# The prefix of a fused attention and feed-forward kernel: transposes on TensorE, another order of its turns, and background tiles placed otherwise

## The chip, the cores and the metric

The kernel runs on the 8 cores of one Trainium2 chip, as one program with other data on each core and no exchange between them. Time is device time of the slowest core, in microseconds (us). A profile is one profiled execution, and its page and trace show the slowest core of it, here core 6, unless another is named. The engines are TensorE (PE; its weight loads are PEld), VectorE (DVE), ScalarE (ACT), GpSimd (POOL) and the sync engine (SP), which only issues DMAs.

## What is computed

A layer on x of shape 4 x 4096 x 1024: layer norm, then a gated recurrence over time (heads of 256), whose result is normalised and multiplied by Wo, plus a feed-forward block with ternary weights; both are added to x.

```python
xn = _layernorm(x)
q, k, v = silu(xn @ Wq.T), silu(xn @ Wk.T), silu(xn @ Wv.T)
f = log_sigmoid(xn @ Wf.T) / 8;  s = 1 - exp(f)
S1[t] = S1[t-1] * exp(f) + k s^T ;  qv = softmax(q S1)
S2[t] = S2[t-1] * exp(f) + s v^T ;  o  = silu(qv S2)
attn = rms_norm(o) * g_w @ Wo.T
ffn  = bitlinear(silu(bitlinear(xn, w_gate)) * bitlinear(xn, w_up), w_down)
out  = x + attn + ffn        # bitlinear: weights to {-1,0,1} times their mean |w|
```

Time is a recurrence, so a core that has the second half of a sequence needs the states S1 and S2 after the first half. Each core owns 2048 rows (`xr`) and has the 2048 rows before them (`xp`; zeros for the first half), from which it computes the states itself. This is the prefix. All weights come as float32 in HBM.

## The kernel before

Rows are worked in tiles of 128: NP = 16 tiles of the prefix, from the last to the first, then NO = 16 own tiles. The program is written as one list of operations for each engine (a `Lane`), in the order in which the Python code calls them, with semaphore waits where an operation needs another's result; each engine plays its list strictly in order. So the place of a call in the code is its place in each engine's queue. `mm` and `tr` are matmul and transpose on TensorE, `act` ScalarE, `ts`, `stt`, `tt` and `cp(dv, ...)` VectorE, `cp(gp, ...)` GpSimd, `dma` and `dmaT` (transpose) DMAs of the sync queue, except those that name `gp`.

Stage A1 (from line 518; the loop at 561, 17 steps, called turns): `ln_load` loads a tile of xp into one of two buffers `xin`; `ln_stats` and `ln_rstd` give mean and 1/std (VectorE, then two tiny ScalarE steps); `a_apply` (539) calls `ln_apply` (364), which normalises to bf16 (`xnb`), transposes by DMA into `xnTa`, the tile's transposed form for all later matmuls, and then issues the load of the tile two further on. In turn i stand: `a_apply(i+2)`; 16 matmuls of F (K = 1024, two halves of 512 columns, pair of PSUM banks i % 2), each waiting for all of `wf_t`; exponential and logarithm of F (`a_sp`); statistics of tile i+3; the load of an eighth of Wk (i < 8) or Wv on the GpSimd queue, with a cast to bf16; then, for j = i-1, four matmuls with triangular matrices that carry the running sum of decays in banks 4 and 5, two exponentials (`a_e0[1]`, `a_ds`) and their product `wall[j]`, 1024 columns on VectorE. Banks 6 and 7 are free.

Stage A2 (660): twice (q = 0, 1, half of the columns each) 17 steps: K and V of tile i (16 matmuls, bank ring 0 to 3, SiLU on ScalarE), four matmuls that add tile i-1 to the states in banks 4 to 7. At the end of each q the four banks are copied to `STf`, two by ScalarE and two by VectorE, and cast by GpSimd. Wq is loaded in its first half.

The background: 200 tiles of 512 KB of the weights (8 of Wo; 96 sums of |w| for the scales; 96 quantised), each loaded to one of four buffers `stg`, worked by VectorE (sums in A1 and A2) or ScalarE (later; a quantised tile is scaled by ScalarE, clipped by VectorE and stored by DMA), and replaced by the load of the tile four further on. `bg(n)` puts n tiles at its place in the queues; `bg_a` only the first step and `bg_b` the second of a quantised one. Before: one in each turn of A1 from 3 on (14), two in each step of A2 but the last (62), nine in each slot of stage B.

Stage B (1217): first the projections of own tile 0 (`F_`, `GS_pe`, `GS_el`, `Q_`, `K_`, `KT_`, `V_`), ahead of them `s1_tr`, the transposes of state S1; then 15 slots, in each the attention of one own tile and the projections of the next, at the end of each of which stands more background; then the feed-forward stage on all 16 tiles.

Of the kernel before, what the change touches and what calls it, by code (L numbers as in the profile page):

```python
# [20 lines left out]
NP = 16  # L21
# [89 lines left out]
def build_nc():  # L111
# [24 lines left out]
    with es:  # L136
        keys = ["pe", "dv", "sc", "gp"]
        slots = {}
        for n in (["x0", "x1", "t0", "t1", "st0", "st1", "st2", "st3", "qs0", "qs1", "qs2", "qs3",
                   "a0", "a1", "o0", "o1", "o2", "o3", "y0", "y1", "q0", "q1", "q2", "q3", "wd", "gw"]  # L140
                  + ["mw%d" % i for i in range(4)]
# [396 lines left out]

        def a_apply(i):
            if i < NP:  # L540
                ln_apply(("p", i), i % 2, xnTc(15 - i), "t%d" % (i % 2))
# [17 lines left out]
        ds_free = None  # L559
        ds_t = None  # L560
        for i in range(NP + 1):
            if i < NP:
# [4 lines left out]
                for h in range(2):  # L567
                    for kc in range(8):
                        p = mm(pr[h].ap, xnTc(c)[:, kc * 128:(kc + 1) * 128],
                               wf[:, kc * 1024 + h * 512:kc * 1024 + (h + 1) * 512],  # L570
                               kc == 0, kc == 7, X[("p", i)]["xnT"], wf_t,
                               pf_tok[i % 2], mark=(kc == 7 and h == 1))
                b = i % 2
                t = act(a_e0[0], pr[2], AF.Exp, p, A[i - 1]["sp"] if i else None,
                        scale=-1.0)
                pf_tok[b] = t
                a["sp"] = act(a_sp[i % 3], a_e0[0], AF.Ln, t, sp_tok[i % 3],
                              bias=1.0)
                if i + 3 < NP:
                    a_stats(i + 3)  # L580
                    a_rstd(i + 3)
                if i < 8:
                    wk_t.append(mixer_weight(wk, ap_wk, i, p))
                else:
                    wv_t.append(mixer_weight(wv, ap_wv, i - 8, p))
            if i >= 1:
# [22 lines left out]
        for c in range(2):  # L609
# [6 lines left out]
        for b in range(2):  # L616
# [3 lines left out]
            banks[6 + b].put()  # L620
# [39 lines left out]
        for q in range(2):  # L660
            kv = {}
# [795 lines left out]
```

How the kernel before makes its waits and increments, by code:

```python
    def play(self, e):  # L61
        for w, fn, inc in self.ops:
            for k, v in w:
                e.wait_ge(self.sems[k], v)
            if fn is None:
                continue
            i = fn(e)
            if inc is not None:
                i.then_inc(self.sems[inc[0]], inc[1])
```

## Time and profile before

| | us |
|---|---|
| median of 3 timed runs (range) | 1528.8 (1525.7 to 1530.0) |
| profiled execution, whole | 1530.8 |
| its span on core 6 | 1529.3 |
| spans of the eight cores | 1508.4 to 1529.3 |
| A1, until the first K matmul | 0 to 150.2 |
| A2, until its last sums | 150.2 to 297.3 |
| projections of own tile 0 until slot 0 | to 328.7 |
| slots 0 to 14 | 328.7 to 836.9 |
| last attention tile, feed-forward | to 1529.3 |

The profile is read by its page first: engine busy shares in 40 slices of 38.2 us. Views of the trace then give the busy time in a stretch, the chain of waits that ended last, single instructions in order of time with what they waited for, and the time from a DMA's issue to its landing. A wait is given behind an instruction as the idle time before it and what ended it.

### The profile page before, as it was taken

What the parts mean: (1) busy time and instruction counts of PE and PEld (TensorE: products, weight loads), DVE (VectorE), ACT (ScalarE), POOL (GpSimd) and SP (SyncE); (2) the same over time, 40 slices, a digit from 0 to 9 for tenths busy, and PEclk for the clock granted to TensorE, in tenths of its full rate; (3) what the DMA queues carried; (4) which work ended last, traced back from release to release, by engine and by line L of the source; (5) the groups of instructions that cost most, each with busy time, mean ns of one, the idle gap of its engine ahead of it and who ended that gap; (6) DMA issues with size and microseconds to landing.
All of it is one profiled execution on the core that took longest, in us unless ns stands there. A gap on an engine that the chain in (4) does not pass through costs nothing.

```text
span 1529.3 us, 24179 instructions; the slowest of 8 cores (1508.4 to 1529.3 us)
## 1 busy us (share of the span) xinstructions
PE 1362.6 (89%) x7996; PEld 702.2 (46%) x7996; DVE 860.9 (56%) x1475; ACT 651.8 (43%) x1082; POOL 193.9 (13%) x225
## 2 busy tenths in 40 slices
PE   3666899888889988888887799999999999999999
PEld 1223344355556555555555344444444444444444
DVE  2454656347775577777776355544554455555543
ACT  2556222357778887787884311111111111111120
POOL 1000000001221111121212011111110111011110
PEclk9889999989999999999999999999999999999999
DMA  8999899706776666767751933233222333332322
GB/s 156 198 206 186 233 251 284 217 3 190 197 225 218 200 182 190 195 202 216 226 177 43 359 94 76 63 76 76 61 59 68 76 77 76 77 63 69 70 54 56
DMA packets 193690, 219.69 MB, mean 144 GB/s; under 512 B 125856, under 2 KB 146336, under 8 KB 192416
## 3 DMA queue, kind: packets, MB, share of 16 engines
q1 hardware_dynamic: 187664, 197.18, 48.2%
q0 software_dynamic: 5904, 20.97, 6.0%
q8 instruction: 66, 1.08, 0.3%
q14 instruction: 56, 0.46, 0.1%
HBM read 167.78 MB, written 29.36 MB: 129 GB/s over the span
## 4 chain that ended last, share of the span: by engine, by line
PE 70%; DMA 11%; DVE 8%; issue 5%; ACT 4%; SPq 1%; POOL 0%; DVEq 0%; ACTq 0%; POOLq 0%
PE ps L265 68%; DMA stg<-wgT 3%; DMA xin<-xp 3%; PE ps L270 2%; DVE STf L299 2%; DMA wf<-wfT 1%; DMA xin<-xr 1%; DMA gu_s<-stB 1%; DMA stg<-wuT 1%; DVE part L418 1%; DVE xnb L291 1%; ACT b_ok L282 1%; DVE b_qt L299 1%; DVE b_ok L285 1%; SPq L310 1%
## 5 line engine op out<-in xcount | busy, mean ns | idle before, releaser
L265 PE MATMUL ps<-wgu,xnTb 128*128 128x512 fp8e4 x2048 | 446.2, 379 | 0.0
L265 PEld LDWEIGHTS ps<-wgu,xnTb 128*128 128x128 bf16 x2048 | 200.5, 98 | 241.2 <-issue 1.0
L282 ACT ACTIVATE sg<-ps,ccol 128x512 f32<-128x512 f32 x128 | 86.1, 684 | 424.0 <-PE ps L265 422.9
L265 PE MATMUL ps<-wd,qT 128*128 128x512 fp8e4 x960 | 209.6, 379 | 0.0
L285 DVE TENSOR_TENSOR gu<-ps,sg 128x512 f32<-128x512 f32 x128 | 88.3, 690 | 190.1 <-PE ps L265 178.6
L265 PEld LDWEIGHTS ps<-wd,qT 128*128 128x128 bf16 x960 | 93.9, 98 | 113.3
L282 ACT ACTIVATE stg<-stg,wsc 128x1024 f32<-128x1024 f32 x96 | 109.6, 1144 | 27.5 <-DMA stg<-wuT 12.8
L265 PE MATMUL ps<-wf,xnTa 128*128 128x512 bf16 x256 | 70.1, 437 | 41.7 <-DMA wf<-wfT 25.2
L418 DVE TENSOR_REDUCE part<-stg 128x1 f32<-128x1024 f32 x64 | 77.6, 1218 | 49.2 <-DMA stg<-wgT 25.1
L303 POOL CAST b_s<-STf 128x512 bf16<-128x512 f32 x64 | 45.8, 719 | 432.6 <-DVE STf L299 319.6
L461 DVE TENSOR_SCALAR stB<-stg 128x1024 fp8e4<-128x1024 f32 x96 | 66.2, 689 | 60.0 <-ACT stg L282 49.7
L1161 DVE TENSOR_REDUCE ccol<-gu 128x1 f32<-128x512 f32 x128 | 87.7, 685 | 14.1 <-DVE gu L285 0.9
L299 DVE SCALAR_TENSOR_TENSOR STf<-STf,dcol,ps 128x512 f32<-128x512 f32 x120 | 87.9, 736 | 0.2 <-PE ps L265 0.2
L285 POOL TENSOR_TENSOR xa<-xa,xin 128x1024 f32<-128x1024 f32 x16 | 37.5, 2347 | 395.9 <-DMA xa<-at_s 395.9
L299 DVE SCALAR_TENSOR_TENSOR ob<-ps,ccol,xa 128x512 f32<-128x512 f32 x32 | 23.9, 748 | 103.2 <-PE ps L265 103.2
L282 ACT ACTIVATE kv<-ps 128x512 bf16<-128x512 f32 x64 | 37.9, 597 | 92.0 <-PE ps L265 92.0
L265 PE MATMUL ps<-wo,b_oT 128*128 128x512 bf16 x256 | 70.3, 424 | 1.1 <-ACT b_wo L282 1.1
L282 ACT ACTIVATE qb<-q 128x1024 bf16<-128x1024 int8 x32 | 33.8, 1057 | 81.1 <-DVE q L289 81.1
L265 PE MATMUL ps<-wk,xnTb 128*128 128x512 bf16 x256 | 65.3, 401 | 0.0
L265 PEld LDWEIGHTS ps<-wf,xnTa 128*128 128x128 bf16 x256 | 26.8, 109 | 82.6 <-issue 63.1
L265 PE MATMUL ps<-xnTb,wq 128*128 128x128 bf16 x1024 | 63.2, 220 | 0.0
L265 PE MATMUL ps<-wk,xnTa 128*128 128x512 bf16 x256 | 62.5, 388 | 0.0
(139 smaller groups left out, 1973.2 us busy)
## 6 DMA issues: line engine op xcount, KB each, us to landing
stg<-wgT SPq DMA_DIRECT2D x64, 512.0 KB, 6.6
stg<-wuT SPq DMA_DIRECT2D x64, 512.0 KB, 6.2
stg<-wdT SPq DMA_DIRECT2D x64, 512.0 KB, 5.3
xin<-xr SPq DMA_DIRECT2D x32, 512.0 KB, 4.5
xin<-xp SPq DMA_DIRECT2D x16, 512.0 KB, 6.4
gu_s<-stB SPq DMA_DIRECT2D x64, 128.0 KB, 5.8
at_s<-b_wo SPq DMA_DIRECT2D x32, 256.0 KB, 2.1
wgu<-gu_s POOLq DMA_DIRECT2D x8, 1024.0 KB, 17.8
```

Of the source, the lines that this page charges most:

```text
L265: return pe(lambda e: e.matmul(out=out, lhsT=lhsT, rhs=rhs, start=start, stop=stop, skip_group_check=True), *toks, mark=mark)
L270: return pe(lambda e: e.transpose(out=out, in_=in_, identity=identb), *toks, mark=mark)
L282: return sc(lambda e: e.activation(out=out, in_=in_, func=func, **kw), *toks)
L285: return lane(lambda e: e.tensor_tensor(out=out, in0=a, in1=b, op=op), *toks)
L291: return lane(lambda e: e.tensor_scalar(out=out, in0=a, scalar1=s1, scalar2=s2, op0=op0, op1=op1), *toks)
L299: return dv(lambda e: e.scalar_tensor_tensor(out=out, in0=a, scalar=s, in1=b, op0=op0, op1=op1, reverse0=rev), *toks)
L303: return lane(lambda e: e.tensor_copy(out=out, in_=in_), *toks)
L310: sp, lambda e: e.dma_start(out=out, in_=in_, transpose=True), *toks)
L418: tk = dv(lambda e: e.tensor_reduce(out=pc, in_=stg[b], axis=AXX, op=ALU.add, apply_absolute_value=True), t)
L461: tp = dv(lambda e: e.tensor_scalar(out=stB[q], in0=stg[b], scalar1=2.0 ** -9, scalar2=-2.0 ** -9, op0=ALU.min, op1=ALU.max, saturate=Fals ...
L1161: dv(lambda e: e.tensor_reduce(out=mx, in_=g, axis=AXX, op=ALU.max, apply_absolute_value=True), tg))
```

## The change

In A1 the normalised tile is transposed by eight transposes on TensorE into banks 6 and 7 (`a_tr`) and copied by VectorE (`a_tc`), instead of by DMA. In turn i stand `a_apply(i+2)`, F of tile i, `a_tr(i+2)`, the exponential; statistics of tile i+3, then `a_w(i-2)`, the decay product of tile i-2 (before: of i-1, at the end of the turn), then the copy `a_tc(i+2)`; logarithm, rstd. Wf is loaded in eight pieces by halves of its columns, the left half first, over eight semaphores, and F waits only for its piece; the left half of turn 1 is computed between the two halves of turn 0. Background tiles stand in A1 from turn 12 on (5) and not from turn 3. A2 is one run of 32 steps, two tiles in each from step 1 on; the states are copied out by ScalarE alone; the last sum, its copies, the casts and two background tiles stand behind F of own tile 0, and `s1_tr` behind its V. A slot has ten background tiles, the tenth at the place of `bg_a(2)`.

```diff
-                  + ["mw%d" % i for i in range(4)]
+                  + ["mw%d" % i for i in range(8)]
...
-            return dma("mw%d" % (n % 4), gp, dst[:, kc * 1024:(kc + 1) * 1024],
+            return dma("mw%d" % (n % 8), gp, dst[:, kc * 1024:(kc + 1) * 1024],
...
-        wf_t = [mixer_weight(wf, ap_wf, kc) for kc in range(8)]
+        def wf_piece(h, q):
...
+            return dma("mw%d" % (n % 8), gp, v3(wf, 8)[:, 2 * q:2 * q + 2, hs],
+                       ap_wf[q * 256:(q + 1) * 256, hs].rearrange("(k p) c -> p k c", p=128))
+
+        wf_h = [[wf_piece(h, q) for q in range(4)] for h in range(2)]
+        wf_t = wf_h[0] + wf_h[1]
...
+        def a_tr(i):
...
+            for kc in range(8):
+                q = tr(banks[6 + b].bf[:, kc * 128:(kc + 1) * 128],
+                       xnb[b][:, kc * 128:(kc + 1) * 128], d["nb"], k2, tr_tok[b],
+                       mark=(kc == 7))
+            xnb_tok[b] = d["trp"] = q
+
+        def a_tc(i):
+            if i < NP:
+                d = X[("p", i)]
+                d["xnT"] = tr_tok[i % 2] = cp(dv, xnTc(15 - i), banks[6 + i % 2].bf, d["trp"])
+
+        def a_f(i, h):
...
+            for kc in range(8):
+                q = mm(pairF[i % 2][h].ap, xnTc(c)[:, kc * 128:(kc + 1) * 128],
+                       wf[:, kc * 1024 + h * 512:kc * 1024 + (h + 1) * 512],
+                       kc == 0, kc == 7, X[("p", i)]["xnT"], wf_h[h][kc // 2],
+                       pf_tok[i % 2], mark=(kc == 7 and h == 1))
+            return q
...
             if i < NP:
-                ln_apply(("p", i), i % 2, xnTc(15 - i), "t%d" % (i % 2))
+                d = X[("p", i)]
+                b = i % 2
+                d["nb"] = ts(dv, xnb[b], xin[b], d["dst"][:, 0:1], ALU.subtract, d["rs"],
+                             xnb_tok[b], s2=d["dst"][:, 1:2], op1=ALU.mult)
+                xin_tok[b] = d["nb"]
...
+            a_tr(i)
+            a_tc(i)
...
+        def a_w(j):
+
+            if j >= 0:
+                w_t[j] = stt(wall[:, (15 - j) * 1024:(16 - j) * 1024], a_e0[1], 1.0, a_ds,
+                             ALU.subtract, ALU.mult, A[j]["w"], rev=True)
+                ds_fr[0] = w_t[j]
...
                 a_apply(i + 2)
+                if i != 1:
+                    a_f(i, 0)
+                if i == 0:
+                    a_f(1, 0)
+                p = a_f(i, 1)
+                a_tr(i + 2)
...
+                if i + 3 < NP:
+                    ln_stats(("p", i + 3), mra[:, ((i + 3) % 4) * 2:((i + 3) % 4) * 2 + 2])
+                a_w(i - 2)
+                a_tc(i + 2)
...
-                if i + 3 < NP:
-                    a_stats(i + 3)
-                    a_rstd(i + 3)
+                a_rstd(i + 3)
...
+            if i == NP:
+                a_w(i - 2)
...
-                e1 = act(a_e0[1], a_sp[j % 3], AF.Exp, sp_j, ds_free, scale=-0.125)
-                ds_t = act(a_ds, pr[2], AF.Exp, p, ds_free, scale=-0.125)
-                w_t[j] = stt(wall[:, (15 - j) * 1024:(16 - j) * 1024], a_e0[1], 1.0, a_ds,
-                             ALU.subtract, ALU.mult, ds_t, e1, rev=True)
-                ds_free = w_t[j]
-            if i >= 3:
+                e1 = act(a_e0[1], a_sp[j % 3], AF.Exp, sp_j, ds_fr[0], scale=-0.125)
+                ds_t = act(a_ds, pr[2], AF.Exp, p, ds_fr[0], scale=-0.125)
+                A[j]["w"] = [ds_t, e1]
+            if i >= 12:
                 bg(1)
-            if i == 2:
+            if i == 10:
                 for k in range(4):
                     bg_load(k)
+        a_w(NP - 1)
...
+        def a2_kv(n):
...
+        def a2_sum(n):
...
+        def a2_out(q, p):
...
-                dst = STf[:, (4 * q + g) * 512:(4 * q + g + 1) * 512]
-                if g % 2 == 0:
-                    t = act(dst, banks[4 + g].ap, AF.Copy, p2, w_t[NP - 1])
-                else:
-                    t = cp(dv, dst, banks[4 + g].ap, p2, w_t[NP - 1])
+                t = act(STf[:, (4 * q + g) * 512:(4 * q + g + 1) * 512], banks[4 + g].ap,
+                        AF.Copy, p, w_t[NP - 1])
...
-        U["s1free"] = p2
-        A2_done = p2
-        for h in range(4):
-            banks[4 + h].put(*s_free[h])
-            s1_cast(h)
-        U["s1free"] = None
...
+        kv = {}
+        for n in range(2 * NP):
+            x2 = a2_kv(n)
+            if n >= 1:
+                p2 = a2_sum(n - 1)
+                if n == NP:
+                    a2_out(0, p2)
+                bg(2)
+                if n <= NP and n % 2 == 0:
+                    wq_t.append(mixer_weight(wq, ap_wq, n // 2 - 1, p2))
+
+        A2_done = x2
...
-        for g in range(2):
-            s1_tr(g, RC)
         for h in range(2):
             F_(0, h)
+        p2 = a2_sum(2 * NP - 1)
+        a2_out(1, p2)
+        U["s1free"] = p2
+        for h in range(4):
+            banks[4 + h].put(*s_free[h])
+            s1_cast(h)
+        U["s1free"] = None
+        bg(2)
         for h in range(2):
             GS_pe(0, h)
             GS_el(0, h)
@@ -1075,6 +1134,7 @@
         for h in range(2):
             KT_(0, h)
             V_(0, h)
+            s1_tr(h, RC)
...
-            bg_a()
+            bg_a(2)
...
-            bg_b()
+            bg_b(2)
```

## Rows read from the trace of the kernel before

**Rows 1.** The page: DMA busy tenths in 40 slices; costliest groups, one of them.

```profile
DMA  8999899706776666767751933233222333332322
...
L282 ACT ACTIVATE stg<-stg,wsc 128x1024 f32<-128x1024 f32 x96 | 109.6, 1144 | 27.5 <-DMA stg<-wuT 12.8
```

**Rows 2.** Busy time by stretch: stretch and its us, engines' busy us, PEclk, DMA share, GB/s.

```profile
42.50:139.30 96.80, 64.66 (x240) 28.12 (x241) 47.51 (x68) 53.63 (x72) 6.33 (x12) 0.88 0.97 206
...
150.20:295.30 145.10, 140.06 (x636) 62.49 (x636) 81.03 (x77) 44.62 (x74) 5.43 (x10) 0.98 0.89 244
295.30:315.60 20.30, 11.46 (x53) 5.58 (x51) 5.29 (x8) 10.09 (x16) 3.45 (x6) 0.75 0.42 126
...
498.08:529.94 31.86, 29.29 (x249) 18.73 (x248) 20.19 (x37) 27.06 (x56) 5.61 (x8) 0.95 0.60 190
...
629.97:666.29 36.32, 29.83 (x250) 18.64 (x248) 25.33 (x46) 27.67 (x47) 6.27 (x8) 0.91 0.72 217
```

**Rows 3.** The chain that ended last, within 0 to 345 us: start, us, what.

```profile
16.04 8.88 DMA wf<-wfT
...
72.67 7.74 DMA xin<-xp
80.50 0.69 DVE lnst L351
...
86.63 0.74 DVE xnb L291
87.48 1.24 SPq L310
88.84 6.38 DMA xin<-xp
```

**Rows 4.** Tile `xin`, 0 to 160 us: from issue to landing.

```profile
DMA to landing us min/median/max: 3.9/6.4/12.5
```

**Rows 5.** Tile `xin`, 866 to 1529 us: from issue to landing.

```profile
DMA to landing us min/median/max: 3.5/3.9/4.3
```

**Rows 6.** Groups, 25 to 150 us: form, count, busy us, mean ns, idle before.

```profile
L299 DVE SCALAR_TENSOR_TENSOR wall<-a_e,a_ds 128x1024 bf16<-128x1024 f32 x15 | 18.4, 1225 | 43.0 <-ACT a_ds L282 43.0
L282 ACT ACTIVATE a_sp<-a_e 128x1024 fp32r<-128x1024 f32 x16 | 16.9, 1057 | 1.5
...
L265 PE MATMUL ps<-a_sp,UT 128*128 128x512 f32 x30 | 13.5, 450 | 21.9 <-ACT a_ds L282 21.9
...
L291 DVE TENSOR_SCALAR xnb<-xin,mra 128x1024 bf16<-128x1024 f32 x14 | 11.3, 807 | 5.1 <-ACT mra L282 5.1
L351 DVE BATCH_NORM_STATS2 lnst<-xin 128x6 f32<-128x512 f32 x14 | 9.7, 690 | 27.3 <-DMA xin<-xp 27.3
```

**Rows 7.** Tile `S1b`: ns min/median/max, first and last start.

```profile
L303 DVE COPY S1b<-ps x32: 674/681/692, 305.2 to 831.7; 128x1024 bf16<-128x1024 bf16 x32
```

**Rows 8.** In order of time, A1 and the start of A2: start, us, operation, wait.

```profile
25.16 9.37 PE L265 MATMUL ps<-wf,xnTa 128*128 128x512 bf16 x32 [25.16 <-DMA wf<-wfT]
...
42.53 5.30 PE L265 MATMUL ps<-wf,xnTa 128*128 128x512 bf16 x16 [2.08 <-DMA xnTa<-xnb]
...
49.19 3.63 PE L265 MATMUL ps<-wf,xnTa 128*128 128x512 bf16 x16
...
139.30 5.18 PE L265 MATMUL ps<-wf,xnTa 128*128 128x512 bf16 x16 [3.43 <-DMA xnTa<-xnb]
...
163.11 1.87 PE L265 MATMUL ps<-kv,wall 128*128 128x512 bf16 x4 [4.57 <-ACT kv L282]
```

**Rows 9.** In order of time, the end of A2.

```profile
295.27 2.02 PE L265 MATMUL ps<-kv,wall 128*128 128x512 bf16 x8
...
301.14 1.28 DVE L303 COPY STf<-ps 128x512 f32<-128x512 f32 x2
...
303.93 2.26 PE L270 MATMUL ps<-identb,b_s 128*128 128x128 bf16 x16 [6.64 <-POOL b_s L303]
...
315.64 2.67 PE L265 MATMUL ps<-xnTb,wq 128*128 128x128 bf16 x31
```

More of the change, by code:

```diff
@@ L566, in build_nc @@
                 a_apply(i + 2)
[L567 to L572, printed above, removed]
+                if i != 1:
[4 more added lines that the diff above has]
+                a_tr(i + 2)
                 b = i % 2
@@ L619, in build_nc @@
             banks[4 + b].put(ds_t)
-            banks[6 + b].put()
+            banks[6 + b].put(tr_tok[b])
         ringP = Ring(banks[0:4])
@@ L658, in s1_tr @@
             s1b_t[2 * g] = s1b_t[2 * g + 1] = t
-        for q in range(2):
-            kv = {}
-            for i in range(NP + 1):
-                if i < NP:
-                    c = 15 - i
-                    res = []
-                    for wt, wtok, o in ((wk, wk_t, 0), (wv, wv_t, 256)):
-                        bk = ringP.take()
-                        for kc in range(8):
-                            p = mm(bk.ap, xnTc(c)[:, kc * 128:(kc + 1) * 128],
-                                   wt[:, kc * 1024 + q * 512:kc * 1024 + (q + 1) * 512],
-                                   kc == 0, kc == 7, wtok, bk.freed, mark=(kc == 7))
-                        t = act(heads(kv2[i % 2], 2, o), v3(bk.ap, 2), AF.Silu, p,
-                                kv_tok[i % 2])
-                        bk.put(t)
-                        res.append(t)
-                    kv[i] = res
-                if i >= 1:
-                    j = i - 1
-                    c = 15 - j
-                    b = j % 2
-                    wc = wall[:, c * 1024 + q * 512:c * 1024 + (q + 1) * 512]
-                    for g in range(4):
-                        p2 = mm(banks[4 + g].ap, wc[:, g * 128:(g + 1) * 128],
-                                kv2[b][:, (g // 2) * 512:(g // 2 + 1) * 512], j == 0,
-                                j == NP - 1, kv[j], w_t[j], s_free[g], mark=(g == 3))
-                    kv_tok[b] = p2
-                    if i < NP or q == 0:
-                        bg(2)
-                    if q == 0 and i % 2 == 0:
-                        wq_t.append(mixer_weight(wq, ap_wq, i // 2 - 1, p2))
@@ new lines, in a2_kv @@
+        def a2_kv(n):
+            q, i = n // NP, n % NP
+            res = []
+            for wt, wtok, o in ((wk, wk_t, 0), (wv, wv_t, 256)):
+                bk = ringP.take()
+                for kc in range(8):
+                    p = mm(bk.ap, xnTc(15 - i)[:, kc * 128:(kc + 1) * 128],
+                           wt[:, kc * 1024 + q * 512:kc * 1024 + (q + 1) * 512],
+                           kc == 0, kc == 7, wtok, bk.freed, mark=(kc == 7))
+                t = act(heads(kv2[n % 2], 2, o), v3(bk.ap, 2), AF.Silu, p, kv_tok[n % 2])
+                bk.put(t)
+                res.append(t)
+            kv[n] = res
+            return p
@@ new lines, in a2_sum @@
+        def a2_sum(n):
+            q, j = n // NP, n % NP
+            c = 15 - j
+            b = n % 2
+            wc = wall[:, c * 1024 + q * 512:c * 1024 + (q + 1) * 512]
+            for g in range(4):
+                p = mm(banks[4 + g].ap, wc[:, g * 128:(g + 1) * 128],
+                       kv2[b][:, (g // 2) * 512:(g // 2 + 1) * 512], j == 0, j == NP - 1,
+                       kv[n], w_t[j], s_free[g], mark=True)
+            kv_tok[b] = p
+            return p
+        def a2_out(q, p):
```

11 lines of the change are left out of this document (10 added, 1 removed).

## The prediction

> **What bounds the kernel now.** I read the page first, for where the DMA is full; then the busy time by stage; then the chain of work that ended last, within the prefix; last the waits and durations of single instructions. The profiled execution took 1530.8 us, with a span of 1529.3 on its slowest core; the median of the three timed runs is 1528.8. The sum below stands against 1530.8, and its 2 us above the median are inside the spread of the runs (1525.7 to 1530.0).
>
> The prefix runs from 0 to about 297 us: stage A1 (16 turns of layer norm, F projection and decay products) until the K projection starts at 150.2, then stage A2 (32 turns of K, V and state sums). In turns 2 to 14 of A1, from 42.5 to 139.3 us, 13 turns take 96.8 us, 7.45 each, while TensorE is busy 64.7 us, VectorE 47.5 and ScalarE 53.6 of them and the DMA share is 0.97 [rows 2]; the page's DMA digits are 8 or 9 over the whole prefix but one slice [rows 1]. No compute engine is the bound: the DMA, or the wait for it, is. The chain shows how. A load of x takes 7.74 us to land, then come the statistics at 80.50, other VectorE work, the normalisation at 86.63, 1.24 us in which the sync queue issues the DMA transpose, and only then the next load at 88.84 [rows 3]. Since each of two buffers has its own such loop, 16.2 us pass for two turns. The reader is to see that the transpose stands ahead of the load in the same queue, and that a background tile (0.75 us of VectorE) and the decay product of the turn before (1.23 us, after a wait for the exponential) stand ahead of the normalisation. A2 is another matter: TensorE is busy 140.1 of 145.1 us there at 0.220 us a matmul [rows 2], so it runs at its floor, and its background loads cost it nothing although the DMA share is 0.89.
>
> **A1, the steady turns.** Per turn the change removes one DMA transpose (1.24 us of the sync queue) and, until turn 12, one background tile with its 0.5 MB load. It adds on TensorE 8 transposes and on VectorE one copy of 1024 columns out of PSUM, 0.68 us [rows 7]. The 16 transposes of the later stage take 2.26 us in a stretch that starts after an idle TensorE [rows 9], so 0.14 each is the upper price; back to back with a busy engine I take 0.06 to 0.14, 0.5 to 1.1 us a turn. The engines' own limits are then: ScalarE four passes of 1024 columns, 1.06 by the costliest [rows 6], at most 4.2, plus two tiny ones and hand-overs, 5.0; VectorE 0.81 for the normalisation, two statistics at 0.69, 1.23 for the decay product, 0.68 for the copy and 0.2 for the aggregate, 4.3 to 4.6; TensorE 3.63 for F [rows 8], 0.5 to 1.1 for the transposes, 1.0 to 1.8 for four decay matmuls (0.45 each is an upper price [rows 6]), 5.1 to 6.5. F took 5.30 us in the turn that starts after a long idle [rows 8], so the upper end is what a slow clock would make of it; the new turns leave TensorE far less idle, and I take 5.2.
>
> The loop of the load sets the rest. With L from issue to landing, VectorE's order for one buffer is: landing, statistics 1.6, decay product 1.23, PSUM copy 0.68, normalisation 0.81, about 0.4 of hand-overs, next load. That is L + 4.8 for two turns. The transposes and the wait for the exponential are out of it, since the product now uses exponentials of the turn before. L was 3.9 / 6.4 / 12.5 us (least, median, most) in the prefix [rows 4], and 3.9 as median in the last stage, where the DMA is a third busy [rows 5]. A turn then moves 0.52 MB of x and 0.52 MB of weights read and written as 0.26; at the 274 GB/s that A2 reaches when full (244 at a share of 0.89 [rows 2]) that is between 2.9 and 3.8 us of DMA in a turn, two thirds of it. So L falls at worst not at all and at best towards 4. I take 6.0 to 6.2, nearer to the median of the same stage than to the quiet stage, because the eight cores load at once here: (6.2 + 4.8) / 2 = 5.5 us a turn. Bounds: 5.2 (the engines) and 6.3 (L = 7.7, the row of the chain). Turns 2 to 14 take 71.5 us for 96.8: **-25.3** (between -29 and -15).
>
> At this point the Trainium skill speaks against the change. Its page "Advanced Engine Details and Errata", section X-Bar Transpose (TRN2), says that transpose DMAs are as fast as regular ones; by that rule taking them out frees the DMA only of their 0.26 MB, a sixth of a turn's traffic. The trace does not agree by itself: A1 at a share of 0.97 moved 206 GB/s, A2 at 0.89 moved 244 [rows 2], though the casting weight loads also lie in the first. By the rule L would stay where it was, which is the first rival below.
>
> **A1, the start.** Now all eight pieces of the F weights must have landed (the last one is issued at 16.04 and takes 8.88 us [rows 3]) before the first matmul at 25.16; the first two turns of F are 9.4 us at the slow pace, and F of turn 2 starts at 42.53 [rows 8]. After, eight pieces go out at once, the left halves first: the left halves of turns 0 and 1 run while the right halves land, and only 8 matmuls wait for the last piece. The bytes (4.2 MB of weights, 2 MB of x) are the same, so I let the last piece land at 23, between 21 (the two transposes are gone) and 25 (as now). The right half of turn 0 ends at 24; exponential, logarithm, rstd and normalisation of tile 3 follow until 28; transposes, and F of turn 2 starts at 30: **-12.5** (-9 to -15). Pieces with shorter rows have no row here; within those bounds.
>
> **From the last F to A2.** F of turn 15 starts at 139.30 and K at 150.20; after it TensorE waits 4.57 us for ScalarE's first SiLU, which is behind the statistics of the first two own tiles [rows 8]. Products, own tiles and one background tile stand there as before, only the last product is issued two steps later, on a VectorE that is not late: **0** (-1 to +3).
>
> **A2.** One run of 32 turns for two runs of 16: what stood at the seam is a wait of 0.5 us of TensorE, for VectorE's copy of the states, which is now ScalarE's: **-0.5**. The background tiles are the same 62 (two in each turn from 1 to 31) with the same eight weight loads, so the same traffic, and the last wait of the F and V weight pieces is covered by the same 10.9 us as now. The four quantised tiles at the end of A2 become sums.
>
> **The end of A2.** Now the last V matmuls end and two sums follow at 295.27, the states are copied until 302.4 (behind a quantised tile whose store VectorE waits for), cast, transposed at 303.93, and Q of the first own tile starts at 315.64 [rows 9]: 20.4 us. After, F of the first own tile follows the last but one sum at once. Call that point T, 296.2 in the old count. F until T+3.5, its exponentials and logarithms on ScalarE until T+5.0 with the table load, the last sum under them; then four state copies of 0.6 (T+7.4) and two background tiles of 1.14 [rows 1] (T+9.7) stand in ScalarE's queue ahead of the gate exponentials, whose second half frees the bank that TensorE's next decay matmul needs: Q starts at T+12.7. Old: 19.4. So 6.7 less, and the two state transposes, 2.2 us with their 16 instructions [rows 9], come back after V: **-4.5** (-6 to +1 if the two tiles' loads are late and hold ScalarE).
>
> **The background debt.** Of 200 tiles 76 were done before the first slot; now 5 in A1, 62 in A2, 2 at its end, 69. Seven more tiles lie in the slots, at ten a slot: 13.1 slots for 13.8. A slot of sums takes 31.86 us, one of quantised tiles 36.32 [rows 2]: 0.50 us for each of nine. Four of the seven are quantised, three are sums: **+3** (0 if the slots have room; +8 at ScalarE's full 1.14 for each, +15 if every slot grows by one such step).
>
> **Sum.** 1530.8 - 12.5 - 25.3 - 0 - 0.5 - 4.5 + 3 = **1491.0 us**. The last stage, from 867 us on, has TensorE 99% busy by the page and isn't touched; it only starts earlier.
>
> **Rivals.** *The load still lands late.* If L doesn't fall, or grows to 8 or 9 because eight cores now ask faster, a turn is 6.3 to 6.9 us and A1 gives back 10 to 18: 1501 to 1509. For it: the longest landing is 12.5, and the skill's rule. Against: the share of 0.97 was the cause that the traffic shows. *The slots pay.* One more ScalarE step in each of 13 slots at full price is 15 us and not 3: 1503; for it speaks that the quantised slots are already 4.5 longer than the others, against it ScalarE's idle fifth. *The gain is given back in A2.* A2's DMA starts with less slack, VectorE runs late through it, and the first own tile waits for it: some 15 us, 1506. Against: the traffic in A2 is the same as now. *Slower.* VectorE takes its queue in order, and the statistics, which wait for the load, now stand ahead of the decay product and the PSUM copy that feeds the next F. With L at 12.5 us, the worst landing of the prefix, a turn is (12.5 + 4.8) / 2 = 8.65, 13 turns take 112.5, the steady part costs +15.7 and the whole comes out at 1532; from L = 12.4 on the kernel is slower than before. Against: the median is half of that with a full DMA.
>
> **How the numbers follow.** Forecast 0.60 (its own range 1481 to 1500); late loads 0.19; slots pay 0.13; given back in A2 0.04; slower 0.03; the last 0.01 is that the saving is below 5 us. The range 1480 to 1509 leaves out a part of the late loads and the tail of the slots on one side, and a turn under 5.2 on the other. A measurement of this kernel can tell 0.3%, 4.6 us, from no change: faster 0.96, same 0.01, slower 0.03.
>
> **What would show it.** F of turn 2 at about 30 us, of turn 15 at 101 to 103, K at 112, the last V matmul near 257, Q of the first own tile 12 to 15 us behind it; turns of 5.5 us with VectorE or TensorE waiting less than 0.5 for x; slots of about 32 and 36 to 37 us with the last tile in slot 13. Wrong if turns are over 6.3 us with VectorE's statistics waiting for x, if the weights' last piece lands after 26, or if the slots grow by over a microsecond each.

## The result, and the profile after

The changed kernel takes **1516.1 us** as median (1514.8 to 1516.9), the kernel before 1529.4 in the same comparison: 0.9931 of it, 95% interval 0.9911 to 0.9951. It is faster by 0.7%, 11 us by the ratio and 13 by the medians, and not by the 38 of the forecast, and it lies above the forecast's range. A time given below is the median of all timed runs of a kernel, some of which fell in a slower state of the chip, and the ratios use the fast runs alone and are what kernels are compared by. The profiled execution took 1515.6 us, with a span of 1514.1 on its slowest core, core 0 (all cores: 1491.1 to 1514.1); that of before had 1529.3 on core 6.

The page of the changed kernel: busy tenths in 40 slices, then the shares by engine of the chain that ended last.

```profile
PE   4978999787888897888887799999999999999999
...
ACT  2863233676788877778864211111111111111120
...
DMA  7878997166765677767603832323322233332322
...
PE 75%; DMA 8%; DVE 6%; issue 5%; ACT 5%; POOL 1%; DVEq 0%; ACTq 0%; SPq 0%; POOLq 0%
```

The DMA digits of the first four slices are 7878 where they were 8999 [rows 1]. Next, busy time by stretch (columns as in [rows 2]): eleven steady turns of A1; the stretch around turn 13; A2 from K on; three slots (0 being the first: 2, 6 and 10).

```profile
34.43:88.66 54.23, 54.10 (x310) 29.14 (x309) 41.22 (x64) 48.03 (x68) 5.83 (x12) 1.00 0.83 178
...
88.66:103.89 15.23, 6.25 (x30) 3.41 (x29) 7.09 (x10) 6.07 (x8) 0.53 (x1) 0.79 0.73 202
...
117.47:261.00 143.53, 139.06 (x640) 62.62 (x639) 80.48 (x76) 44.34 (x76) 5.41 (x10) 0.99 0.89 258
...
357.04:395.58 38.54, 29.82 (x249) 18.65 (x248) 26.03 (x47) 27.56 (x47) 6.25 (x8) 0.96 0.73 204
...
500.83:532.78 31.95, 28.02 (x249) 18.21 (x248) 19.56 (x37) 27.64 (x57) 5.60 (x8) 1.00 0.62 197
...
640.99:678.53 37.54, 30.74 (x249) 19.14 (x248) 27.02 (x48) 28.22 (x48) 5.80 (x8) 0.91 0.67 225
```

In the steady turns TensorE is busy 54.10 of 54.23 us, 4.93 us a turn: the loop of the load is no longer the bound, TensorE is. In order of time (start, us, operation, wait), A1 after:

```profile
15.62 5.29 PE L265 MATMUL ps<-wf,xnTa 128*128 128x512 bf16 x16
...
28.64 1.01 PE L265 MATMUL ps<-wf,xnTa 128*128 128x512 bf16 x2 [1.82 <-DMA wf<-wfT]
...
34.43 3.63 PE L265 MATMUL ps<-wf,xnTa 128*128 128x512 bf16 x16
...
88.66 3.63 PE L265 MATMUL ps<-wf,xnTa 128*128 128x512 bf16 x16
...
96.42 0.69 DVE L351 BATCH_NORM_STATS2 lnst<-xin 128x6 f32<-128x512 f32 x1 [10.26 <-DMA xin<-xp]
...
101.26 1.01 PE L270 MATMUL ps<-identb,xnb 128*128 128x128 bf16 x8 [8.98 <-DVE xnb L291]
```

The one hole in A1 is at 92 to 101 us: VectorE's statistics wait 10.26 us for a load of x. The sync queue at that place, and the chain's step:

```profile
76.85 3.23 SPq L306 DMA_DIRECT2D stg<-woT  x4
...
81.38 0.33 SPq L306 DMA_DIRECT2D xin<-xp  x1
...
81.38 14.94 DMA xin<-xp
```

The four first background loads go out together (`if i == 10`), and the load of x behind them takes 14.94 us to land; the landings of `xin` in the prefix are 3.4/4.8/14.9 us, where they were 3.9/6.4/12.5 [rows 4]. The end of A2, in order of time:

```profile
261.00 3.61 PE L265 MATMUL ps<-wf,xnTb 128*128 128x512 bf16 x16
...
271.68 0.76 PE L265 MATMUL ps<-b_sp,SL 128*128 128x512 f32 x1 [5.04 <-ACT b_df L282]
...
273.81 3.60 PE L265 MATMUL ps<-xnTb,wq 128*128 128x128 bf16 x32
```

**Where the time went.** The first slot starts (F of the next own tile) at 288.3 us on core 0, against 328.7 on the slowest core of before: -40.4. The 14 slots that hold background tiles then take 495.4 us against 471.1: +24.3. From there to the end it is 730.4 against 729.5: +0.9. The sum, -15.2, is the difference of the spans. Busy time of the 14 slots on those two cores, first before, then after:

```profile
328.70:799.80 471.10, 404.97 (x3453) 260.08 (x3452) 336.28 (x613) 373.98 (x670) 84.66 (x112) 0.95 0.66 196
...
288.30:783.70 495.40, 416.17 (x3456) 264.27 (x3454) 341.40 (x619) 381.06 (x680) 81.92 (x112) 0.93 0.64 195
```

Of the 24.3 us, 13.1 are idle time of TensorE (79.2 for 66.1), and 11.2 are the same matmuls taking longer (416.2 for 405.0), at a granted clock of 0.93 for 0.95. Since two slowest cores are compared there, the table takes the start of K, the start of slot 0 and the length of the 14 slots in each of the eight cores, and gives the medians over cores:

| us, median of 8 cores | K starts | slot 0 starts | 14 slots together |
|---|---|---|---|
| before | 147.8 | 325.4 | 462.8 (457 to 471) |
| after | 116.3 | 284.8 | 489.6 (480 to 496) |
| difference | -31.5 | -40.6 | +26.8 |

Slot by slot, medians before: 32.8 34.0 34.6 33.6 31.7 **31.5 31.5 32.6** 33.2 34.2 33.3 33.9 33.4 32.4; after: 32.7 34.6 37.0 36.0 36.0 **32.0 31.6 32.7** 37.2 36.6 37.2 34.7 35.6 33.5. The three in bold are as long as before: slots 5 and 6 hold sums (6 ends with one or two quantised tiles), slot 7 quantised tiles. What grew, by up to 4.3 us, are slots 1 to 4 and 8 to 13. Most of them hold quantised tiles, but slot 4, which grew most, holds only sums in both kernels. What those that grew have in common is that the slot before them holds quantised tiles, which reads as a lateness carried from slot to slot; no run tests that. The medians are of one profiled execution each: a second one of the changed kernel (e14) has slot 0 at 286.4 and 491.9 us for the 14 slots, so a difference of 2 us in them says nothing.

### The profile page after: what moved, and what is told of

Same layout as the page of the kernel before. It is cut to its first block, busy times and chain, and to the rows that moved or that the text cites. A ratio compares the mean times of both kernels' runs of the same rounds, so it can differ in the third digit from the quotient of the medians.

```text
span 1514.1 us, 24442 instructions; the slowest of 8 cores (1491.1 to 1514.1 us)
## 1 busy us (share of the span) xinstructions
PE 1370.8 (91%) x8124; PEld 714.7 (47%) x8124; DVE 864.4 (57%) x1482; ACT 659.5 (44%) x1096; POOL 192.6 (13%) x225
## 4 chain that ended last, share of the span: by engine, by line
PE 75%; DMA 8%; DVE 6%; issue 5%; ACT 5%; POOL 1%; DVEq 0%; ACTq 0%; SPq 0%; POOLq 0%
PE ps L265 73%; PE ps L270 2%; DMA stg<-wgT 2%; DMA stg<-wdT 2%; DVE STf L299 1%; DMA wf<-wfT 1%; ACT stg L282 1%; DMA xin<-xp 1%; DMA stg<-wuT 1%; DMA xin<-xr 1%; ACT L281 1%; ACT b_ok L282 1%; DVE stB L461 1%; DVE b_qt L299 1%; DVE b_ok L285 1%
## 5 line engine op out<-in xcount | busy, mean ns | idle before, releaser
L282 ACT ACTIVATE stg<-stg,wsc 128x1024 f32<-128x1024 f32 x96 | 109.8, 1144 | 32.9 <-DMA stg<-wgT 12.2
L418 DVE TENSOR_REDUCE part<-stg 128x1 f32<-128x1024 f32 x59 | 71.6, 1219 | 49.2 <-DMA stg<-wgT 30.5
L285 POOL TENSOR_TENSOR xa<-xa,xin 128x1024 f32<-128x1024 f32 x16 | 37.5, 2346 | 394.6 <-DMA xa<-at_s 394.6
L265 PE MATMUL ps<-wo,b_oT 128*128 128x512 bf16 x256 | 75.4, 447 | 1.1 <-ACT b_wo L282 1.1
L265 PE MATMUL ps<-wf,xnTa 128*128 128x512 bf16 x256 | 62.6, 397 | 5.5 <-DMA wf<-wfT 5.5
L265 PE MATMUL ps<-wf,xnTb 128*128 128x512 bf16 x256 | 61.1, 383 | 6.0 <-ACT b_KV L282 5.9
L265 PEld LDWEIGHTS ps<-xnTb,wq 128*128 128x128 bf16 x1024 | 61.7, 101 | 4.1 <-issue 0.5
```

Source lines behind the costliest of these rows:

```text
L265: return pe(lambda e: e.matmul(out=out, lhsT=lhsT, rhs=rhs, start=start, stop=stop, skip_group_check=True), *toks, mark=mark)
L282: return sc(lambda e: e.activation(out=out, in_=in_, func=func, **kw), *toks)
L285: return lane(lambda e: e.tensor_tensor(out=out, in0=a, in1=b, op=op), *toks)
L418: tk = dv(lambda e: e.tensor_reduce(out=pc, in_=stg[b], axis=AXX, op=ALU.add, apply_absolute_value=True), t)
```

## The experiments

The prefix as a whole had given what was forecast, so the question was the slots: why does one more tile in each cost 2 us? The theories: the price lies in the two **passes** of the tile (ScalarE, VectorE), which stand ahead of the kernel's own work in queues played in order; in its **load**, which competes with the loads of the slot; in the **place** in the queue where the tenth stands; or it isn't the tenth at all, but the **prefix**, whose earlier end shifts the slots against each other. Ratios are to the kernel before, with their 95% interval.

**Nine a slot** (e1). Five tiles go back into A1, where they start from turn 7.

```diff
-            if i >= 12:
+            if i >= 7:
...
-            if i == 10:
+            if i == 5:
...
-            bg_a(2)
+            bg_a()
...
-            bg_b(2)
+            bg_b()
```

> The changed kernel with nine background tiles in a slot as before, and the five tiles that this leaves over in A1 (one in each turn from 7 on, first loads at turn 5). Theory 1, the tenth tile of a slot costs what the prefix gained: the 14 slots take 471 us again for 495, the five more tiles in A1 cost at most 1 us each, and the time is 1492 to 1498 us. Theory 2, the slots are longer for another reason that comes with the earlier start (the traffic of the eight cores, the order of the first own tile): the slots stay at 495 and the time is 1514 to 1520.

Measured: **1497.0 us, 0.9783 (0.9757 to 0.9809)**. K starts at 116.2, slot 0 at 287.1, the slots take 466.6. So the tenth tile costs 23 us in the slots, and five tiles in A1 cost 2.3 us, hardly more than two executions of one kernel differ by. By the ratios the two kernels are 0.0148 to 0.0153 apart (e14), 23 us.

**The old prefix with ten** (e2). The same two edits of a slot, the other way round, in the kernel before.

```diff
-            bg_a()
+            bg_a(2)
...
-            bg_b()
+            bg_b(2)
```

> The kernel before with the tenth tile in each slot at the same place, its prefix untouched; the tiles end in slot 12 for slot 13. Theory 1 (the tenth tile costs about 1.8 us a slot whatever the prefix is): 1545 to 1553 us. Theory 2: within 3 us of the kernel before.

Measured: 1551.0 us, 1.015 (1.013 to 1.017). The slots take 483.6 us for 462.8, with the prefix as it was. The theory that the new prefix makes the slots longer falls.

**The tenth elsewhere** (e3). Its passes stand at other places of the slot.

```diff
             GS_el(f, 0)
+            bg_a()
...
             up(c, 3)
-            bg_b()
+            bg_b(2)
...
-            bg_a(2)
+            bg_a()
...
-            bg_b(2)
+            bg_b()
```

> The changed kernel with ten tiles a slot, but the tenth in the first half of the slot, between the gate exponentials and the output projection, where ScalarE waited 1.4 us for TensorE; its clip stands behind the fourth state update. If the place is at fault (six tiles follow each other within 14 us and the last ones wait for their loads, which keeps the SiLU of V and so a bank from TensorE): 1495 to 1503 us. If the amount is (one more pass of ScalarE and its successors in a slot, anywhere): 1512 to 1518.

Measured: 1510.6 us, 0.9875 (0.9854 to 0.9896); slots 484.1. That lies between the two expectations: the place is worth a part of the 23 us, 5.5 by the slots and 9 by the ratios, not the most of it.

**Nine and a pass of ScalarE** (e4), at the tenth's place, over constants; no load.

```diff
+            if s < NO - 2:
+                sc(lambda e: e.activation(out=v3(padt, 8), in_=onesf.unsqueeze(1).to_broadcast([128, 8, 128]), func=AF.Copy), A2_done)
```

> As the kernel with nine tiles a slot, and at the place of the tenth a ScalarE pass of 1024 columns over constants, about 1.1 us, without load, clip or store, in slots 0 to 13. Nothing of the computation is changed. If ScalarE's time at that place is the cost: 15 to 22 us above the kernel with nine, 1510 to 1518. If it is the wait for the tenth tile's load: 0 to 6 us above it, 1494 to 1502.

Measured: 1496.4 us, 0.9796 (0.9778 to 0.9813), slots 468.3: not to be told from e1.

**Half the bytes** (e5), with all ten tiles and their passes in place, from tile 73 on.

```diff
+            hc = 512 if k >= 73 else 1024
+            loads[k] = dma("st%d" % (k % 4), sp, stg[k % 4][:, 0:hc], src[:, 0:hc],
+                           stg_tok[k % 4])
```

> The changed kernel, ten tiles a slot, with only the left half (256 KB) of each background tile loaded from tile 73 on; the passes over the buffers stay whole, so the right halves of those weights are not those of the reference. If the slots are long because the tiles' loads land late in a ring of four buffers: the slots come back to about 33 to 34 us, 1488 to 1500. If they are long for the work of the tenth tile on the engines: at most 5 us below the changed kernel, 1511 to 1517.

Measured: 1485.3 us, 0.9701 (0.9666 to 0.9735), slots 460.7: shorter than with nine whole ones, and the time is below the range expected. The kernel leaves out half of each background tile's load. Tile `stg` from 290 us on, issue to landing, and ScalarE's waits for it (sum, count, longest), first e5:

```profile
DMA to landing us min/median/max: 2.3/3.9/7.4
...
ACT stg L282 <- DMA stg<-wgT: 3.5, 2, 2.1
```

The same of the changed kernel:

```profile
DMA to landing us min/median/max: 3.3/5.7/10.4
...
ACT stg L282 <- DMA stg<-wdT: 13.2, 15, 1.7
ACT stg L282 <- DMA stg<-wgT: 12.2, 7, 4.3
ACT stg L282 <- DMA stg<-wuT: 12.1, 9, 3.3
```

These three rows sum to 37.5 us in the changed kernel, 29.1 before and 9.5 with half the bytes (the medians over the eight cores are 31.5, 19.6 and 7.2). All passes of the ten tiles are there in e5, so they can't be the 23 us by themselves. But e5 halves all ten loads, so it doesn't price the tenth.

**Nine and both passes** (e6): e4, and a pass of VectorE over 1024 columns that waits for ScalarE's, at the place of the tenth's.

```diff
+            if s < NO - 2:
+                U["pad"] = dv(lambda e: e.tensor_scalar(
+                    out=pad3, in0=one3, scalar1=2.0 ** -9, scalar2=-2.0 ** -9,
+                    op0=ALU.min, op1=ALU.max), tq)
```

> Nine tiles a slot, and in slots 0 to 13 the tenth tile's work on the engines without its load and store: a ScalarE pass of 1024 columns at its place and a VectorE clip of 1024 columns, which waits for the pass, at the place of its clip. The computation is complete. If load and buffer are the cost: 0 to 6 us above nine a slot, 1494 to 1502. If it is VectorE's or both engines' time: 1507 to 1518.

Measured: 1499.2 us, 0.9809 (0.979 to 0.9828); slots 469.8. The passes are worth 4 us by the ratios, but the intervals of e1 and e6 overlap, so it may be nothing.

**Nine and the traffic** (e11): e1, and two loads of 256 KB a slot into a buffer that nobody reads; no pass. The first of the two is shown; it stands in the queue ahead of the own tile's normalisation and transpose, not behind them as the text below says.

```diff
+            if s < NO - 2:
+                U["padt"] = dma("pad", sp, padf, ap_wg[(s % 8) * 128:(s % 8) * 128 + 128,
+                                                 0:512], A2_done)
```

> Nine tiles a slot, and in slots 0 to 13 two further loads of 256 KB each, together the tenth tile's 512 KB, into a pad that nobody reads, one behind the normalisation of the own tile and one at the place of the tenth tile. Nothing waits for them. If the tenth tile costs by its traffic (all loads land later, eight cores share the memory): 10 to 20 us above nine a slot, 1505 to 1517. If it costs by the turn of the ring of four buffers, where ScalarE waits in line for a load issued late: 0 to 4 us above it, 1495 to 1501.

Measured: 1509.0 us, 0.9854 (0.9827 to 0.988); slots 476.0. Tile `stg` in e11, issue to landing, and ScalarE's waits for it:

```profile
DMA to landing us min/median/max: 3.1/6.3/12.1
...
ACT stg L282 <- DMA stg<-wuT: 18.4, 7, 4.8
ACT stg L282 <- DMA stg<-wdT: 16.9, 10, 4.9
ACT stg L282 <- DMA stg<-wgT: 15.4, 4, 6.0
```

Nobody waits for the added loads, yet the tiles that are waited for land later. In e1 they land in 3.2/5.5/9.1 us, and the same three waits sum to 24.8 us, here to 50.7. That is the slowest core, where it shows most: as medians over the eight cores a tile lands in 6.0 us for 5.6, the longest in 10.2 for 9.1, and the waits sum to 31.2 for 23.1. Each added load also takes the sync queue 0.41 us to issue (median), and e11 doesn't separate that from its bytes.

**Both together** (e13): e11, with the passes again (two of 512 columns on each engine).

> Nine tiles a slot, and in slots 0 to 13 all parts of a tenth except its place in the ring of four buffers: two loads of 256 KB that nobody waits for, a ScalarE pass (two of 512 columns, about 0.1 us dearer) and a VectorE clip (two of 512) at the tenth's places. Alone the passes cost 2 to 4 us and the loads 10 to 12 over nine a slot. If the parts add up and the ring costs the rest: 1508 to 1512, with the changed kernel 4 to 8 us above it. If the parts together make all of the tenth tile's cost (a slot that is fuller everywhere): 1513 to 1519, as the changed kernel.

Measured: 1513.5 us, 0.9889 (0.9863 to 0.9915); slots 482.4. By the ratio it is 1512 us, at the upper end of the first expectation, so it hardly decides between the two by itself.

**The changed kernel once more** (e14), beside these.

> The changed kernel itself, on the same chip as the kernel with all parts of a tenth tile, for their comparison: 1513 to 1519.

Measured: 1520.1 us, 0.9936 (0.9913 to 0.9959), 1 us above what was expected; slots 491.9. The 23 us of the tenth tile are thus: passes 0.0026 x 1529 = 4 us (e6 - e1), load 11 us (e11 - e1), both together 16 us (e13 - e1). From there to the real tile are 7 more (0.9936 - 0.9889), which I put down to its place in the ring of four buffers, since a real tile also holds a buffer and its pass waits for a load. That last part is argued: the intervals of e13 and e14 just overlap, and a real quantised tile also has its store of 128 KB in its own slot, which e13 does not add, so the store is a rival that no run tests.

**The first loads spread** (e7): e1, with the four first background loads in turns 3 to 6, one in each.

```diff
-            if i == 5:
-                for k in range(4):
-                    bg_load(k)
+            if 3 <= i < 7:
+                bg_load(i - 3)
```

> Nine tiles a slot and ten in A1 as before, but the first four background loads are issued one in each of turns 3 to 6 behind that turn's load of x, and not four together in turn 5. In the changed kernel the load of x behind the four took 14.9 us to land and TensorE waited 9 us once. If the four together cause it, the stall goes: 5 to 9 us below nine a slot, 1486 to 1491. If the background traffic as such does, within 3 us of it.

Measured: 1493.4 us, 0.9762 (0.9739 to 0.9785); K starts at 113.1 for 116.2. TensorE's longest wait in the turns, first of e1, then of e7 (start, us, operation, wait):

```profile
77.33 1.01 PE L270 MATMUL ps<-identb,xnb 128*128 128x128 bf16 x8 [8.04 <-DVE xnb L291]
```

```profile
71.22 0.61 PE L270 MATMUL ps<-identb,xnb 128*128 128x128 bf16 x8 [1.86 <-DVE xnb L291]
```

The hole is gone, and the longest landing of `xin` falls from 14.0 to 9.1 us, so the burst made it. The total is above the 1486 to 1491 expected and can't be told from e1's.

**More tiles in A1** (e12): nine a slot, 13 tiles from turn 4 on, first loads in turns 1 to 4.

```diff
+            if i >= 4:
...
+            if 1 <= i < 5:
+                bg_load(i - 1)
```

> Nine tiles a slot and thirteen in A1 (one in each turn from 4 on), the first four loads spread over turns 1 to 4; the three tiles fewer leave the last slot shorter. A tile in A1 cost about 0.6 us and one in a slot 2 to 3. If both hold: 1488 to 1494. If A1's traffic makes x late again, or the gain is taken by the slots: 1494 to 1500.

Measured: 1500.1 us, 0.9796 (0.9773 to 0.9819). A miss, no faster than e1: the slots are 3.4 us shorter (463.2), but slot 0 starts 2.7 us later. VectorE's wait for x in A1 (sum, count, longest) is back:

```profile
DVE lnst L351 <- DMA xin<-xp: 18.1, 9, 5.3
```

**DMA transposes** (e8). The changed kernel with A1's transposes by DMA again, directly behind the normalisation.

```diff
         def a_tr(i):
...
-            if i >= NP:
-                return
+            return
...
         def a_tc(i):
-            if i < NP:
+            if False:
...
+                d["xnT"] = xnb_tok[b] = dmaT("t%d" % b, v3(xnTc(15 - i), 8), v3(xnb[b], 8),
+                                              d["nb"])
```

> The changed kernel with the transposes of A1 by DMA as before, all else kept (order, weight pieces, no background before turn 12). In the changed kernel a turn of A1 takes 4.90 us where nothing waits for x. If the transposes in the sync queue and on the DMA set the old pace: turns of 5.8 to 6.5 us, K at 125 to 137 us for 117, 1524 to 1535. If the background tiles and the order did: turns of 4.9 to 5.2, 1512 to 1520.

Measured: 1533.5 us, 1.0048 (1.0025 to 1.0071), as the first theory expected. K starts at 127.3 for 116.3, slot 0 11.6 us later, and the steady turns take some 6 us for 4.9. Waits in A1 (sum, count, longest), the landings of `xin`, and a steady stretch of A1 in e8:

```profile
DVE lnst L351 <- DMA xin<-xp: 27.6, 9, 7.7
PE ps L265 <- ACT a_ds L282: 15.1, 7, 3.3
...
DMA to landing us min/median/max: 4.3/6.6/14.2
...
45.00:110.00 65.00, 51.21 (x208) 23.70 (x209) 36.27 (x53) 46.05 (x64) 6.21 (x11) 0.94 0.94 197
```

The like stretch of the changed kernel:

```profile
45.00:100.00 55.00, 47.16 (x266) 24.90 (x263) 36.31 (x56) 40.67 (x58) 5.28 (x10) 0.98 0.82 182
```

With the transposes on the DMA, x lands in 6.6 us for 4.8, and a DMA share of 0.94 moves 197 GB/s, where 0.82 moves 182 without: 210 against 222 GB/s for a full share (the two stretches hold much the same work, not quite). This bears on the rule of the Trainium skill's page "Advanced Engine Details and Errata", section X-Bar Transpose (TRN2), that transpose DMAs are as fast as regular ones. The rates of the two stretches differ by 6% over all traffic, which neither proves nor refutes the rule, since the transposes are only a part of the bytes. What the prediction made of the rule, that L would then stay where it was, is refuted: x lands 1.8 us sooner (medians over the cores 4.6 for 6.0).

**The product in the same turn** (e9). The changed kernel with the decay product at the end of its own turn, as before.

```diff
-                a_w(i - 2)
                 a_tc(i + 2)
...
                 A[j]["w"] = [ds_t, e1]
+                a_w(j)
...
-        a_w(NP - 1)
```

> The changed kernel with the decay product in the turn that makes its exponentials, as before (VectorE waits for them at the end of each turn). If that wait was part of the old pace: turns of 5.3 to 6.0 us, 6 to 15 us above the changed kernel, 1521 to 1531. If TensorE at 4.9 us a turn covers it: within 3 us, 1513 to 1519.

Measured: 1536.9 us, 1.0066 (1.0037 to 1.0095), above what was expected, and so are its steady turns (6.2 to 6.8 us, by core). K starts at 130.6, 14.3 us later, slot 0 17.6 later. One turn of TensorE in e9, then two waits in A1:

```profile
48.94 3.63 PE L265 MATMUL ps<-wf,xnTa 128*128 128x512 bf16 x16
...
54.48 0.61 PE L270 MATMUL ps<-identb,xnb 128*128 128x128 bf16 x8 [1.91 <-DVE xnb L291]
...
DVE wall L299 <- ACT a_ds L282: 29.3, 13, 3.2
...
PE ps L270 <- DVE xnb L291: 18.2, 11, 4.3
```

VectorE waits 2.3 us for the exponential in each of 13 turns, with the normalisation of the next tile behind it, and TensorE waits for that.

**The weights in whole pieces** (e10). The changed kernel with Wf in eight pieces of whole rows, all awaited by the first matmul.

```diff
-            return dma("mw%d" % (n % 8), gp, dst[:, kc * 1024:(kc + 1) * 1024],
+            return dma("mw%d" % (n % 4), gp, dst[:, kc * 1024:(kc + 1) * 1024],
...
-        wf_h = [[wf_piece(h, q) for q in range(4)] for h in range(2)]
-        wf_t = wf_h[0] + wf_h[1]
+        wf_t = [mixer_weight(wf, ap_wf, kc) for kc in range(8)]
+        wf_h = [[wf_t] * 4] * 2
```

> The changed kernel with F's weights in eight whole pieces over four semaphores, all awaited by the first matmul, as before. If the pieces by halves bring the start: F of turn 2 at 38 to 42 us for 34.4, 4 to 7 us above the changed kernel, 1519 to 1523. If only the transposes that are gone did, F of turn 2 at 35 to 37 and 0 to 3 us above it.

Measured: 1523.4 us, 0.9976 (0.9964 to 0.9988). F of turn 2 starts at 38.17 for 34.43, since the first matmul waits until 25.17 (in order of time):

```profile
25.17 8.14 PE L265 MATMUL ps<-wf,xnTa 128*128 128x512 bf16 x24 [9.36 <-DMA wf<-wfT]
...
38.17 3.63 PE L265 MATMUL ps<-wf,xnTa 128*128 128x512 bf16 x16
```

Slot 0 starts 5.4 us later. The parts of the prefix, each undone alone, cost 11.6 (e8), 17.6 (e9) and 5.4 us (e10), 34.6 together, or 29.8 if slot 0 is counted from e14's 286.4. That this comes near the 40.6 us of the prefix doesn't show that the parts add up; the end of A2, the seam and the nine fewer tiles in A1 were not tried alone.

## Why the prediction was wrong, point by point

The prediction misread a row, which moves time between its first two terms. Turns 0 and 1 are the 32 matmuls at 25.16 [rows 8], and F of turn 2 of the kernel before is this row, which stands between them and the one at 42.53:

```profile
34.85 3.63 PE L265 MATMUL ps<-wf,xnTa 128*128 128x512 bf16 x16
```

So 42.53 is turn 3, and the stretch from 42.5 to 139.3 us holds twelve turns (its 240 matmuls are twelve times 20). They take 8.07 us each and not 7.45, half of the chain's 16.2 us for two turns [rows 3]. The sum isn't touched, since the start has too much by what the turns have too little: counted from 34.85 the same forecast is -4.9 for the start and -32.9 for turns 2 to 14, together the -37.8 of the two terms.

- **The start** (-4.9, counted so): -0.4. F of turn 2 starts at 34.43 and not at 30 (medians over the cores 32.8, and 35.9 before: -3.1). The order is as described; the size was off because the last piece lands at 28.6 and not at 23. In e10, with whole rows and four of the eight pieces at a time, the last piece landed at 25.17; so the new form of the load (half rows, eight pieces at once) makes it later, not earlier. Which of its two sides does, no run told. The pieces by halves help all the same, because work starts before the last one: e10 has F of turn 2 at 38.17, later than before.
- **The steady turns** (-32.9, counted so): -30.4. A free turn is 4.93 us and not 5.5, because L fell further, to a median of 4.8, than the 6.2 I took. The loop of the load is then (4.8 + 4.8) / 2 = 4.8 us a turn, and TensorE's own 4.9, which I had at 5.1 to 6.5, became the bound. Eleven such turns (54.2 us), one of 15.2 and one of 4.6 make 74.1 for the 71.5 forecast. The step that I left out is the burst of four background loads in one turn: I counted its bytes as gone until turn 12 and not its place in the sync queue ahead of a load of x. e7 takes it away, and the hole with it.
- **From the last F to K** (0): 9.0 us for 10.9, -1.9, just outside its bounds of -1 to +3.
- **A2** (-0.5): K to F of the own tile 143.5 us, for 146.0 to the prediction's point T: -2.5. The mechanism is right; A2 runs at TensorE's floor, 139.1 busy, and the rival that gives the gain back there is out.
- **The end of A2** (-4.5): Q starts 12.8 us behind F of the own tile at 261.0, 12.7 forecast from T; with what follows until slot 0 it is -5.2. Right, with the forecast wait: TensorE stands 5.04 us for the gate exponentials, behind the copies and tiles in ScalarE's queue.
- **The background debt** (+3): **+24.3 on core 0, +26.8 as median. This is the step that failed.** The sum came so far to -42.8 at slot 0 against -40.4 measured, and a debt of 3 would have made 1493 of it. That it comes so near is in part luck: the start and the turns gave 7.0 us less than forecast, the other three terms 4.6 more. I took the difference between a slot of quantised tiles and one of sums, divided by nine, 0.50 us, as the price of one more tile. That is an average, and of the difference between two kinds of tile, in slots of nine; the tenth costs 1.7 us a slot (23.4 us from e1 to e14, by 14), or 1.9 against before (26.8 by 14). The average hides that nine sums in a slot cost nothing: such slots take 31.5 us, and so does slot 13 of e2, which has no tile left. And I multiplied it by the seven tiles that moved, when the edit adds a tile to each of 13 slots. What the early end of the background gives back in the changed kernel is nothing: its slot 13 has one tile for nine before, and takes 33.5 us for 32.4. Two of the prediction's signs of being wrong came true, a last piece after 26 us and slots longer by over a microsecond.
- **The bounds and the rival of it.** "+15 if every slot grows by one such step" had the right form, and its rival (*the slots pay*, 1503) the right mechanism, with a chance of 0.13. Its price was wrong too: 1.14 us of ScalarE a slot. Passes without a load cost 0.3 us a slot (e6), the load that the bound left out 0.8 (e11), a real tile 1.7. ScalarE's idle fifth was real; its waits for the loads of background tiles grew (31.5 us for 19.6, medians over the cores).
- **The load still lands late, and slower**: both out. The landings fell in the median, though the longest rose from 12.5 to 14.9 and cost the hole. The Trainium skill's rule is weighed under e8.

The end of slot 2 and the start of slot 3 in the changed kernel, in order of time:

```profile
395.58 1.89 PE L265 MATMUL ps<-wf,xnTb 128*128 128x512 bf16 x8
396.81 1.15 ACT L282 ACTIVATE stg<-stg,wsc 128x1024 f32<-128x1024 f32 x1 [4.27 <-DMA stg<-wgT]
398.62 1.15 ACT L282 ACTIVATE stg<-stg,wsc 128x1024 f32<-128x1024 f32 x1 [0.66 <-DMA stg<-wgT]
399.67 0.58 ACT L282 ACTIVATE b_KV<-ps 128x512 bf16<-128x512 f32 x1
400.39 2.73 PE L265 MATMUL ps<-wf,xnTb 128*128 128x512 bf16 x8 [2.03 <-ACT b_KV L282]
```

ScalarE stands 4.27 us in front of a background tile whose load isn't there. Behind two such tiles in its queue is the copy `b_KV`, which frees the bank that F needs, so TensorE stops between the halves of F, and the second half then takes 2.73 us for the first one's 1.89. Such stops for `b_KV` sum to 5.9 us on core 0 and to 0 to 4.0 on the others, and there are none before or in e1, so they are a part of the price; TensorE's other waits that grew, on the two slowest cores, are for VectorE's `b_qt` (45.6 us for 39.6) and `b_at` (6.0 for 0.8). Such a wait for a load that is filler lands on the critical engine because the queues keep their order.

The best of the kernels tried with all of the work are e1 and e7, 1497.0 and 1493.4 us, 0.978 and 0.976 of before, faster than both kernels: the new prefix as it is, with nine tiles a slot.

## What to carry to other kernels

The price of one more piece of filler is not the average price of those already there: look for the wait it adds where the filler's load and the critical copies share a queue, and multiply it by every slot that gets one, not by the pieces moved. Count a background tile's bytes before its passes, and issue prefetches one by one, not in a burst ahead of a load that somebody waits for. A serial loop through a load can be shortened by taking out of it what belongs to another turn; that was the part of the prefix that cost most when undone (e9). And before a stretch is divided by a number of turns, count its instructions.

## What the runs showed of the hardware

- A load of x behind a burst of four loads of 512 KB on the same queue landed in 14.94 us, three times the median of 4.8. In e1 the longest landing was 14.0 us with such a burst, and in e7, with one background load a turn, 9.1.
- 512 KB more in a slot of some 34 us, read by nobody, raised the landings of the other background tiles from 5.6 to 6.0 us (median) and from 9.1 to 10.2 (longest; both as medians over the eight cores of e1 and e11) and cost 0.8 us a slot, on a DMA whose share from 300 to 700 us is 0.68 to 0.72 in e11. A share well below 1 didn't make a load free.
- Eight transposes of 128x128 on a running TensorE took 0.61 us together, and 1.01 us behind the hole of 9 us. The granted clock was 1.00 in the steady turns (the level of 2.4 GHz throughout), where it was 0.88 before, and F took 3.63 us in each.
